# A graph and feed-forward kernel on Trainium2: register loads one slab early in the first stage

## The reference, cut to what matters

```python
src = concat([s, d, loop]); dst = concat([d, s, loop])   # 21250 edges, sorted by dst
x = x + _L0_gnn_ref(_layernorm(x), W1, b1, Wg, bg, src, dst)

def _L0_gnn_ref(feat, W1, b1, Wg, bg, row, col):
    x1 = feat @ W1 + b1
    deg = segment_sum(ones, col); dis = clip(deg, 1.0) ** -0.5
    gnn = x1
    for k in range(4):
        alpha = tanh(gnn[col] @ Wi + gnn[row] @ Wj + bg[k])
        gnn = gnn + segment_sum(dis[row] * dis[col] * alpha * gnn[row], col)
    return concat([x1, gnn])
```

## Time and profile before

| | us |
|---|---|
| median of 3 runs | 1480.81 |
| lowest, highest | 1480.35, 1481.11 |
| the profiled execution | 1478.62 |
| its span in the trace | 1476.8 |
| out(0) to out(9), the nine periods of the first stage | 43.55 to 150.75 |

### The profile page before, as it was taken

How to read it: one execution, slowest core, us unless ns; L and a number is a source line. 1 busy time by engine, 2 the same in 40 slices (tenths; PEclk the granted TensorE clock), 3 DMA queues, 4 the chain that set the end, 5 groups by cost and what they waited for, 6 DMA issues and landing times.

```text
span 1476.8 us, 28271 instructions
## 1 busy us (share of the span) xinstructions
PE 1412.0 (96%) x8327; PEld 723.6 (49%) x8327; DVE 892.1 (60%) x2053; ACT 545.3 (37%) x758; POOL 357.8 (24%) x373
## 2 busy tenths in 40 slices
PE   6889999999999999999999999999999968999996
PEld 5334444545445444444654444446544435666653
DVE  7888889686988888442433222223347776676652
ACT  4578757373633553111111120001111124465641
POOL 4332320202201120000776002800012311442232
PEclk9999999999999999999999999999999989999998
DMA  7242010000257656462423443520046746889863
GB/s 286 44 87 51 8 44 14 14 14 28 71 156 192 175 142 199 134 166 72 157 71 100 99 108 121 185 100 29 0 144 178 206 179 207 239 246 278 271 165 57
DMA packets 156675, 185.96 MB, mean 126 GB/s; under 512 B 106172, under 2 KB 107659, under 8 KB 156600
## 3 DMA queue, kind: packets, MB, share of 16 engines
q1 hardware_dynamic: 144440, 143.07, 32.4%
q0 software_dynamic: 12160, 41.95, 11.1%
HBM read 118.40 MB, written 41.94 MB: 109 GB/s over the span
## 4 chain that ended last, share of the span: by engine, by line
PE 67%; DVE 16%; issue 8%; DVEq 3%; ACT 2%; DMA 2%; POOL 1%; ACTq 0%; SPq 0%; POOLq 0%
PE ps L1354 25%; PE ps L1425 11%; PE ps L1589 7%; PE ps L1609 6%; PE ps L1254 3%; PE ps L1256 3%; PE ps L1255 3%; PE ps L1615 1%; PE ps L1577 1%; DVE wa L2031 1%; ACT th L1693 1%; DVE hm L2070 1%; DVE sc L2447 1%; DVE bstat L571 1%; DVE cr L2414 1%
## 5 line engine op out<-in xcount | busy, mean ns | idle before, releaser
L1354 PE MATMUL ps<-wa,tb 128*128 128x512 f16 x960 | 208.8, 379 | 0.0
L1425 PE MATMUL ps<-adj,nm 128*128 128x384 f16 (+2 forms) x960 | 169.6, 340 | 0.0
L1254 PE MATMUL ps<-gp,hop 128*128 (+1 forms) x400 | 151.6, 379 | 1.0 <-DVE gn L2144 1.0
L1255 PE MATMUL ps<-gp,hop 128*128 (+1 forms) x400 | 151.6, 379 | 0.0
L1256 PE MATMUL ps<-gp,hop 128*128 (+1 forms) x400 | 151.6, 379 | 0.0
L1354 PEld LDWEIGHTS ps<-wa,tb 128*128 (+1 forms) x960 | 93.3, 98 | 111.3
L1425 PEld LDWEIGHTS ps<-adj,nm 128*128 x960 | 93.9, 98 | 75.4
L1803 ACT ACTIVATE tb<-cx 128x384 f32 (+1 forms) x48 | 26.8, 559 | 273.2 <-DVE cx L2372 273.2
L1354 PE MATMUL ps<-wa,hop 128*128 128x512 f16 x480 | 105.3, 379 | 2.9 <-DVEq L2319 2.9
L1354 PE MATMUL ps<-wb,hop 128*128 128x512 f16 x480 | 105.4, 383 | 0.0
L1589 PE MATMUL ps<-tkT,wb 128*128 128x314 f16 x768 | 103.8, 297 | 1.5 <-ACT tkT L1876 1.5
(11 more groups left out here) (401 smaller groups left out, 2195.5 us busy)
## 6 DMA issues: line engine op xcount, KB each, us to landing
w_st<-in_ew SPq DMA_DIRECT2D x16, 2048.0 KB, 11.0
self_d<-cr SPq DMA_DIRECT2D x20, 512.0 KB, 3.0
cr<-self_d SPq DMA_DIRECT2D x20, 512.0 KB, 3.3
stage<-in_wn POOLq DMA_DIRECT2D x16, 512.0 KB, 3.9
x_d<-cr SPq DMA_DIRECT2D x10, 512.0 KB, 4.9
cx<-x_d SPq DMA_DIRECT2D x10, 512.0 KB, 4.6
cr<-x_d SPq DMA_DIRECT2D x10, 512.0 KB, 4.2
out<-cr SPq DMA_DIRECT2D x10, 512.0 KB, 3.5
```

The source lines that it names most:

```text
L1254: pe.matmul(acc, wh, gh, start=(s_ == 0), stop=False, skip_group_check=True)
L1255: pe.matmul(acc, wh, gl, start=False, stop=False, skip_group_check=True)
L1354: ins = pe.matmul(ps[:, b + c, :], lhs(part, k), w[:, w_, k, c * 512:(c + 1) * 512], start=(k == 0 and part == 0 and w_ == 0), stop=(last ...
L1425: ins = pe.matmul(ps[:, 6 + j, 0:n], nm[:, part, s_, bass.ds(f * P, P)], adj[:, s_, t0 * TP:t0 * TP + n], start=first, stop=(s_ == NT - 1 ...
```

## The change

Three things are moved; no instruction on data is added or removed.

- The load of a slab's first chunk (and the register move that follows from it) is no longer at the head of its `groups`. It stands at the tail of the `groups` of the slab ahead, behind that one's six comparisons. The load of the number of visits goes from the head of `visits(w)` to the tail of `groups(w)`. So two loads stand behind each `groups`, and none ahead of `groups` or `visits`.
- `stats` no longer makes the sequencer wait for its end. `aggregates` does (`settle`). The aggregates of tiles 4 to 6 (t = 1) and 7 to 9 (t = 4) come behind the first `visits` of the period instead of directly behind the statistics.
- `low_a(2)` comes directly behind `stats(4, 6)` at t = 0, instead of behind `visits(2)` and `groups(3)`.

```diff
     def link(self, ins):
         ins.then_inc(self.sem, 1)
         self.at, self.local = self.at + 1, self.local + 1
+        self.eng.wait_ge(self.sem, self.at)
+
+    def mark(self, ins):
+        ins.then_inc(self.sem, 1)
+        self.at, self.local = self.at + 1, self.local + 1
+
+    def settle(self):
         self.eng.wait_ge(self.sem, self.at)
...
-                link(ins)
+                step.mark(ins)

             def aggregates(n):
                 v.sem_inc(s_tick, 1)
+                step.settle()
...
+            first_of, visits_in = {}, {}
+
+            def begin_at(w):
+                first_of[w] = v.value_load(lohi[0:1, 0, w:w + 1], min_val=0, max_val=NCH - GC - GV)
+                v.reg_mov(at_chunk[w % 3], first_of[w] + GC)
+
             def groups(w):
                 j = w % 3
-                first = v.value_load(lohi[0:1, 0, w:w + 1], min_val=0, max_val=NCH - GC - GV)
...
-                edge_marks(first, GC, oh_d[j], w).then_inc(s_ohd, 1)
-                v.reg_mov(at_chunk[j], first + GC)
+                edge_marks(first_of[w], GC, oh_d[j], w).then_inc(s_ohd, 1)
+                visits_in[w] = visits_of(v, w)
+                if w + 1 < NWIN:
+                    begin_at(w + 1)

             def visits(w):
                 j = w % 3
-                with v.Fori(0, visits_of(v, w)):
+                with v.Fori(0, visits_in[w]):
...
-            split_v1(), groups(0), visits(0), groups(1), visits(1), groups(2)
+            split_v1(), begin_at(0), groups(0), visits(0), groups(1), visits(1), groups(2)
...
                 if t == 0:
-                    stats(4, 6)
+                    stats(4, 6), low_a(2)
                 if t == 1:
-                    stats(6, 7), aggregates(2).then_inc(s_agg, 1)
+                    stats(6, 7)
                 if t in (2, 3, 4):
                     stats(5 + t, 6 + t)
-                if t == 4:
-                    aggregates(3).then_inc(s_agg, 1)
                 for w in WINDOWS[t]:
                     if w + 2 < NWIN:
                         visits(w + 2)
+                    if t in (1, 4) and w == WINDOWS[t][0]:
+                        aggregates(1 + (t + 2) // 3).then_inc(s_agg, 1)
                     if w + 3 < NWIN:
                         groups(w + 3)
-                    if w == WINDOWS[t][0] and t + 2 < NT:
+                    if w == WINDOWS[t][0] and 2 < t + 2 < NT:
                         low_a(t + 2)
```

## The result

| | before | after |
|---|---|---|
| median | 1480.81 | 1471.69 |
| lowest, highest | 1480.35, 1481.79 | 1470.97, 1474.71 |
| the profiled execution | 1478.62 | 1471.68 |
| its span | 1476.8 | 1469.8 |

The ratio is 0.9949 (0.9936 to 0.9962): 0.5% faster, or 7.5 us. The two medians alone give 9.1 us and the profiled pair 6.9; single executions of one kernel scatter by several us. A second measurement, in the last group of experiments, gave 0.9927 (0.9909 to 0.9946). One execution of the loads alone (1512.51) and one of the kernel before in the last group (1665.26) had a far lower mean clock than the others of their kernel, and stand in no ratio and no median here.

What follows compares the result with a forecast made beforehand. Neither VectorE nor TensorE is full; VectorE's sequencer was taken to leave the gaps, bounding late periods. Terms sum to -6.55 against the profiled 1478.62, giving 1472.1; taken from the median, 2.2 higher, 1474.3. Range 1470.5 to 1481.0.

Steps and rivals of the forecast that it cites:

- ahead of out(0): Slabs 0 to 2: sequencer-bound, two more loads stand here, less the existing lead: +0.55 us, bounds 0 and +1.5.
- t = 0: out(0) to out(1): VectorE's gaps of 1.24 and 0.72 go, about 0.4 comes back ahead of out(1): -1.6 us.
- t = 1: out(1) to out(2): gaps of 1.6 go, GpSimd's interference moves a period on, tile 2 starts earlier: -2.0 us.
- t = 2: out(2) to out(3): GpSimd's instruction holds VectorE's comparisons where the gap was, add_x(1) comes on top: 0.
- t = 3: out(3) to out(4): GpSimd's interference again takes the gap's place, but without the addition: -0.7 us.
- t = 4: out(4) to out(5): gaps of 1.6 go and GpSimd's interference moves to the next period: -2.0 us.
- t = 5: out(5) to out(6): sequencer-bound at 10.8, takes the previous period's GpSimd interference on top of its own: +1.0 us.
- t = 7 and 8: out(7) to out(9): sequencer-bound with TensorE close behind, 24.4 us together: -0.3 us.
- 1 (-2.5): Sequencer bounds nearly everywhere; moved loads show as 0.5 ahead of low part and out, t = 1 to 5: 1478.3, chance 0.24.
- 2 (slower): Loads ahead of low_a delay transposes and so TensorE, in t = 1 to 8: +3.3 us, 1484.1, chance 0.10.
- 3 (swallowed): From t = 5 TensorE waits for visits at GpSimd's pace, so the early gain becomes idle time: -0.7, 1480.1, chance 0.11.
- 4 (-9.8): Both reduced-clock stretches (tile 2, t = 5) get full clock, returning 1.9 and 1.4; VectorE keeps its lead: 1471.0, chance 0.13.

Runs made afterwards that it cites:

- the link alone: Kernel before with only VectorE's sequencer wait behind the statistics removed and aggregates behind the first visit; loads and low_a(2) unmoved: 1475.39 us, ratio 0.9968.
- a short add_x: Kernel after, with GpSimd adding 8 of 512 columns of x1 to x, the rest of that sum left out: 1466.84 us, ratio 0.9910.
- ScalarE's other order: The fastest kernel, with ScalarE making the high part of tile t + 2 ahead of the slab's source side: 1468.45 us, ratio 0.9924.
- the fastest kernel: Kernel after, with one load fetching both numbers of a slab into two registers, so 25 of 50 loads go: 1467.02 us, ratio 0.9910.

## Why the forecast came true, and where its steps did not

The forecast was 1474.3, in a range of 1470.5 to 1481.0, and 1471.69 came. What it rests on, that VectorE's sequencer leaves gaps and that the moved loads and the removed wait close them, is shown by the loads alone and the link alone. **The sum** was -6.55 against the profiled execution, and the profiled pair gave -6.94. **The step from the sum to the median** failed: it assumed that the changed kernel's profile would lie 2.2 below its median as that of before did, and it lies on it (1471.68 and 1471.69). Hence the 2.6: 0.4 of the sum and 2.2 of this. Which of the two differences is the truer is not settled by one execution each. By the last group the medians differ by 10.6 (1480.27 and 1469.70), while its profiled execution, 1472.26, again stands 6.4 below that of before; the stage's end moved by 7.06 and 6.70. The part of the program behind the stage scatters by as much (last section).

That the sum hit is in part luck. Its terms, against the two timelines, add up to -7.6, which is where the first products of the hops stand (158.96 to 151.35); the profiled total has 6.9 of it:

| | forecast | measured | |
|---|---|---|---|
| ahead of out(0) | +0.55 | +0.46 | 43.55 to 44.01 |
| t = 0 | -1.6 | -2.13 | both gaps gone, none new ahead of out(1) |
| t = 1 | -2.0 | -3.19 | gaps gone, GpSimd's meeting moved to t = 2 |
| t = 2 | 0 | -0.11 | GpSimd in the gap's place |
| t = 3 | -0.7 | +0.79 | tile 4 late and at the lower clock |
| t = 4 | -2.0 | +0.22 | high part late, GpSimd still there |
| t = 5 | +1.0 | -0.98 | the meeting stayed in t = 4 |
| t = 6 | -1.0 | -1.42 | |
| t = 7 and 8 | -0.3 | -0.70 | |
| to the end of the stage | -0.5 | -0.56 | |

- **t = 0 and 1**: right in kind, 1.7 too small together. The 0.4 that was to come back ahead of out(1) did not: six comparisons at 51.48 run straight into out at 53.27 with two loads behind them, so there the lead suffices. At t = 1 gaps of 1.6 went, 2.08 of busy time went with the meeting (10.16 to 8.08), and a gap of 0.52 is new. The choice between 9 and 10.8 was for a tile 2 that might meet the lower clock again; products began at 52.89 rather than 54.5 and ran in 5.34, so out(2) waited for nothing. The full clock itself gave no time back: before, out(2) at 66.73 followed VectorE's own work without a gap, and with the low part alone, where tile 2 has the full clock, t = 1 is as long as before.
- **t = 2**: the step that looked least likely is the best borne out. The gap went and GpSimd stood in it (2.09 and 1.20 for 0.60 and 0.41), the link put back costs 0.2, and a short add_x takes 1.5 off. Here a rule of the Trainium skill (GPSIMD Engine Reference, "Key points": GpSimd shares its SBUF interfaces with VectorE) agrees with the trace. The page names two kinds of VectorE instruction that are held up; which of them these comparisons are, no run here shows. Taken alone it gave -4 for the whole change, and -6.94 was measured: most closed gaps don't lie beside GpSimd.
- **t = 3**: the step "the same, without the addition" failed. VectorE's gaps of 2.20 went and 0.63 came back as busy time beside GpSimd, as forecast in kind, but then out(4) waited 2.36 for tile 4. The step looked at VectorE only and didn't ask what the earlier work does to TensorE. By the trace tile 4's products begin 7.07 us behind the start of its low part (68.35 to 75.42) where tile 2's take 5.89 (47.00 to 52.89), and they take 7.04, in part at the lower clock, as tile 2's did before. The low part alone showed the same one tile earlier, at tile 3. Without the early low part t = 3 takes 10.17 and not 10.99. So the rows show where part of the gain of t = 1 was given back. Why the clock falls at one tile and not at another stays open: it fell behind waits of 3.68 before, 1.84 with the low part alone, 2.29 after and 2.12 with ScalarE's other order, but the fastest kernel waits 1.17 and 1.88 at tiles 3 and 4 and keeps 2.4 GHz, and without the early low part it waits 3.71 at tile 2 and keeps it too. The length of the wait alone doesn't decide it.
- **t = 4**: the meeting with GpSimd was to move on to t = 5 and it didn't, because VectorE itself was held up by the high part (2.09) and came as late as before against GpSimd. The forecast named what waits for `low_a` if the high part is late, and checked it at t = 0 only. This miss of 2.2 and the one of 2.0 at t = 5 have this one cause, with opposite signs, and so cancel in the sum.
- **t = 5 to 8**: -3.1 for a forecast of -0.3. The loads alone give -3.04 there and the link alone -0.58. This is the term that was mis-sized. That the sequencer bounds these periods is right (an added load costs 0.54, and its own length is 0.52 with a step of 0.02), but moving the loads was taken for worthless there, and 10.8 for three slabs is too much: t = 8 has three and takes 10.28. Before, visits and groups stood behind their own loads, with gaps of 0.2 to 1.2 by "issue"; with the loads at the tail, part of them seems to run beside the comparisons even here. No run separates that further.
- **The length of a load.** The Trainium skill (DMA: Bandwidth & Descriptors, "Latency and other measured facts") puts the floor of a tensor load at about 600 ns. The kernel after has 50 with medians of 0.308 (lowest 0.298), and 0.5 to 0.6 is what an added load costs with its arithmetic. The measurement decides, and -3 by the page's figure was less than what came.

**The rivals.** 1 (-2.5) is true of the late periods and of the time ahead of out(0). In t = 0 to 4 two loads a slab leave 0.7 of gaps and a third makes it 3.0, so there the sequencer isn't the bound, but it is close to it. 2 (slower) didn't come: "issue" stands ahead of no low part; with 25 more loads in the kernel after it does (0.8), and that kernel is slower than before, 1.0031. 3 (swallowed) is wrong: out(5) is 3.96 us early (98.84 to 94.88) and out(9) 7.06. 4 (-9.8) priced the two slow stretches at 1.9 and 1.4. Tile 2 got its clock and so did t = 5 (0.86 to 1.00), but one stretch is at t = 3 instead. And the prices were wrong in kind: before, VectorE was busy up to out(2) and out(6), so no time hung on the slow tiles there. The stage is wholly at full clock with one load fewer, with and without the early low part, and with the small add_x; with ScalarE's other order it isn't. **The signs** that were named: "issue" 9.4 of a forecast under 10; out(1) 53.27 for 54, out(5) 94.88 for 93, out(9) 143.69 for 145. Of the signs against it, gaps of 0.5 and more ahead of low part and out, there is none ahead of a low part, but out has four by "issue" (2.1 in all, 0.44 to 0.61).

**Two readings of the prediction** don't hold as they stand. "No other engine is late" was read from the first row of its table alone; the row with 2.2 for TensorE is answered above. And the 16.9 of that row are of 34 to 156 us, the 18.0 of idle time of out(0) to out(9), so one isn't a share of the other.

## What to carry to other kernels

Ask of an engine's idle time by "issue" what its sequencer was doing, and put register loads behind the instructions that fill the queue, not ahead of them; where two numbers lie side by side, one load of both is worth more still (6.3 in the stage here, for 3.7 by the loads' move). When a change closes gaps on one engine, go through the periods once more for each other engine that will now be late, ScalarE's and TensorE's part included, since a stall or a low clock taken from one tile may only go to another. A slow instruction costs nothing where nobody waits for its end, so look for the gap behind it before pricing it. Judge such a change by its stage's own timeline, and give the total with an interval.

## What the runs showed of the hardware that was not expected

**A filled queue hides two loads a slab, and not a third.** In the kernel after, t = 0 to 4 hold 20 loads of 0.31 us with 0.19 of arithmetic each, and VectorE is idle there for 0.7 us apart from its waits for TensorE and ScalarE. Ten more loads bring that to 3.0. In the kernel before, where the loads stand ahead and a link empties the queue, VectorE's idle time in t = 0 to 4 is 9.68 us, and ten more loads make it 14.26.

**GpSimd beside a 16-bit comparison.** Two comparisons that take 0.60 took 2.09 beside 32-bit instructions of GpSimd of 1.2 to 1.3, with the next two instructions 1.20 for 0.41; six took 3.47 for 1.63. VectorE thus lost 2.28 of the 3.16 us that GpSimd ran beside the four (63.67 to 66.83), and 1.84 of 2.56 beside the six (91.48 to 94.04): about 0.7 of GpSimd's time in both.

**What lies behind the stage scatters as much as the change gives.** From VectorE's instruction bcur<-pcol (2.5 us behind out(9)) to the end of the span these kernels do the same, but for one load ahead of visits(24). It takes 1323.5 us in the kernel before and 1323.6 after, but 1320.2 with the loads alone and 1328.2 in the kernel before with the added load. These windows are of the loads alone and then of before with one more load, a hundred us that begin 1020 behind that instruction, and the whole rest:

```profile
1169.54:1269.54 100.00, 86.02 (x740) 50.04 (x739) 73.16 (x203) 38.09 (x40) 23.36 (x22) 0.91 0.63 198
149.54:1469.70 1320.16, 1283.16 (x7592) 657.19 (x7590) 768.15 (x1683) 446.21 (x538) 307.96 (x233) 0.99 0.44 128
```

```profile
1183.57:1283.57 100.00, 84.83 (x711) 47.77 (x710) 70.39 (x204) 35.12 (x34) 21.63 (x22) 0.86 0.59 182
163.57:1491.80 1328.23, 1289.28 (x7590) 660.71 (x7590) 770.08 (x1683) 446.70 (x537) 308.35 (x233) 0.98 0.43 127
```

The granted clock in these hundred us is 0.91 in the first and 0.86 in the second, and in the other kernels it lies between or at these. At 0.90 and 0.91 the rest takes 1320.2 to 1323.5, at 0.88 it takes 1323.6 to 1325.9, at 0.86 1323.8 to 1328.2. A different start isn't needed for such differences: the six executions of the kernel after in the last group took 1466.17 to 1472.26, with a mean granted clock of 0.992 over the whole program in the shortest and 0.987 in the longest. So a total that differs by 2 us from the stage's gain, as in "loads only" (-3.73 in the stage, -5.4 by the medians), needs no cause in the change. Whether the start of the program has a part in it as well is not shown.
